# A constant row moved to PSUM in a gather-heavy graph layer

## The reference

```python
s_u = x @ W_u.T + b_u
s_v = x @ W_v.T
e = s_u[src] + s_v[dst]
e = jnp.where(e >= 0, e, 0.2 * e)
m = jax.ops.segment_max(e, dst, num_segments=n_nodes)
e_exp = jnp.exp(e - m[dst])
denom = jax.ops.segment_sum(e_exp, dst, num_segments=n_nodes)
probs = e_exp / denom[dst]
xh = x.reshape(n_nodes, head_dim, num_heads)
msg = xh[src] * probs[:, None, :]
out = jax.ops.segment_sum(msg, dst, num_segments=n_nodes)
```

## Time and profile before

| what | value |
|---|---|
| median of 3 runs | 4693.43 us (4681.35 to 4693.45) |
| profiled execution | 4686.26 us, its span 4684.5 us |
| POOL busy | 3468.7 us, 74% of the span |
| PE busy | 3095.6 us, 66% |
| DVE busy | 2213.4 us, 47% |
| mean granted TensorE clock | 0.814 of full |
| gathers of layer 1 (L1466) | 880, mean 1181 ns |

### The profile page before, as it was taken

How to read it: one execution, slowest core, us unless ns; L and a number is a source line. 1 busy time by engine, 2 the same in 40 slices (tenths; PEclk the granted TensorE clock), 3 DMA queues, 4 the chain that set the end, 5 groups by cost and what they waited for, 6 DMA issues and landing times. The chain is left out here.

```text
span 4684.5 us, 61408 instructions
## 1 busy us (share of the span) xinstructions
PE 3095.6 (66%) x13554; PEld 1900.7 (41%) x13555; DVE 2213.4 (47%) x5019; ACT 908.4 (19%) x2810; POOL 3468.7 (74%) x2948
## 2 busy tenths in 40 slices
PE   2548777877777777777777776884545555555541
PEld 1224444444444444444444443552333333443331
DVE  2553333333333333333333332995766667766665
ACT  0212222222222222222222222332000000000002
POOL 4237888888888888888888886775777777777764
PEclk9768888889888888888889897996777767667765
DMA  8667666667666667666667666565443434444431
GB/s 300 168 235 176 125 132 134 133 126 138 129 133 125 133 131 135 124 133 130 135 125 131 133 133 132 177 202 172 115 113 109 113 113 114 114 112 114 114 102 63
DMA packets 471759, 641.52 MB, mean 137 GB/s; under 512 B 173607, under 2 KB 365635, under 8 KB 467886
## 3 DMA queue, kind: packets, MB, share of 16 engines
q0 software_dynamic: 198144, 339.26, 38.1%
q1 hardware_dynamic: 245994, 254.83, 18.2%
q10 hardware_dynamic: 27588, 47.08, 3.1%
HBM read 448.23 MB, written 192.71 MB: 137 GB/s over the span
## 5 line engine op out<-in xcount | busy, mean ns | idle before, releaser
L935 POOL DMA_INDIRECT S<-l_msum,l_sink x784 | 1284.8, 1639 | 254.2 <-issue 213.0
L1466 POOL DMA_INDIRECT l_feats<-X_rows,l_gsrc x880 | 1039.2, 1181 | 326.9 <-issue 264.6
L918 POOL DMA_INDIRECT l_ga<-A_rows,l_gsrc x784 | 789.7, 1007 | 265.6 <-issue 160.0
L1008 PE MATMUL l_psU<-l_hid,l_same 128*128 128x257 f32 x1568 | 585.9, 459 | 535.6 <-ACT l_hid L1044 505.3
L981 PE MATMUL l_psC<-l_table,l_onehot 128*128 x4728 | 727.4, 295 | 0.0
L1532 PE MATMUL l_psU<-l_feats,l_same 128*128 128x264 f32 x1760 | 553.5, 478 | 169.5 <-DVE l_feats L1701 124.6
L1048 ACT COPY l_msum<-l_psU 128x257 f32<-128x257 f32 x784 | 292.6, 373 | 1889.9 <-POOLq L934 1313.6
L974 PE MATMUL l_psC<-W1cT,l_attrT 64*128 64x256 f32 x1576 | 623.4, 479 | 13.0 <-DMA l_table<-B_rows 13.0
L981 PEld LDWEIGHTS l_psC<-l_table,l_onehot 128*128 128x128 bf16 x4728 | 426.1, 104 | 367.9 <-issue 306.0
L1008 PEld LDWEIGHTS l_psU<-l_hid,l_same 128*128 128x128 f32 x1568 | 267.4, 214 | 666.2 <-ACT l_hid L1044 579.0
L1532 PEld LDWEIGHTS l_psU<-l_feats,l_same 128*128 128x128 f32 x1760 | 409.0, 240 | 306.9 <-issue 216.8
(11 more groups left out here) (346 smaller groups left out, 3390.7 us busy)
## 6 DMA issues: line engine op xcount, KB each, us to landing
l_srcb<-src_rows SPq DMA_DIRECT2D x99, 512.0 KB
l_locb<-lo_rows SPq DMA_DIRECT2D x55, 512.0 KB
S<-su_zeros ACTq DMA_DIRECT2D x24, 1156.5 KB
l_locb<-loc_rows SPq DMA_DIRECT2D x99, 256.0 KB
nd_sums<-S SPq DMA_DIRECT2D x196, 128.5 KB, 2.2
l_attr<-in_edge_attr SPq DMA_DIRECT2D x98, 256.0 KB
GH_rows<-l_hidden SPq DMA_DIRECT2D x49, 384.0 KB
nd_hidden<-GH_rows SPq DMA_DIRECT2D x49, 384.0 KB, 3.1
```

The source lines that it names most:

```text
L918: pool.indirect_dma_start(ga[:, s, :], None, D["A"], bass.IndirectOffsetOnAxis(ap=gsrc[h][:, j % HALF:j % HALF + 1], axis=0)).then_inc(gat ...
L935: pool.indirect_dma_start(D[f"S{j % NTAB}"], bass.IndirectOffsetOnAxis(ap=sink[j // HALF][:, j % HALF:j % HALF + 1], axis=0), msum[:, j % ...
L1008: nc.tensor.matmul(psU[j % 2][:, 0:UW], same[j // HALF][:, j % HALF, :], hid[:, j % RING, :], start=True, stop=True).then_inc(agg_done, 1)
L1466: pool.indirect_dma_start(feats[r][:, t, :], None, D["X1"], bass.IndirectOffsetOnAxis(ap=gsrc[r][:, t:t + 1], axis=0)).then_inc(gathered[r ...
```

## The change

The constant row is copied once, at the start of layer 1, from SBUF into the first 128 columns of a new PSUM bank `psW` (the eighth), and `find_edge` reads its first operand there. Its second operand, its output and its shape stay. The weight products (L1701) still read both operands from SBUF. Nothing else in the program is added, removed or put in another order; in the changed file the lines behind the new tile lie one to three further down.

```diff
--- before.py
+++ after.py
@@ -1388,6 +1388,7 @@
         psE = m.ps("psE", [P, 512])
         psM = m.ps("psM", [P, 512])
         psV = m.ps("psV", [P, 512])
+        psW = m.ps("psW", [P, 512])
         psU = [m.ps(f"psU{q}", [P, 512]) for q in range(4)]
         keys_in, tables_ready, table_split = m.sem("keys_in"), m.sem("tables_ready"), m.sem("table_split")
         loc_in = [m.sem(f"loc_in{r}") for r in range(SETS)]
@@ -1405,6 +1406,7 @@
         block = st.enter_context(nc.Block())
 
         ENDS, CARRY, SHRINK = P, P + 2 * GROUP, P
+        column = psW[:, 0:P]
 
         def groups(engine, body):
 
@@ -1578,7 +1580,7 @@
                 nc.vector.tensor_scalar(onehot[:, :, :], locb[r][:, :, :], K["winid"][:, 0:1], None, ALU.is_equal).then_inc(onehot_ready, 1)
 
             def find_edge(g):
-                nc.vector.tensor_tensor(same[:, :, :], K["column"][:, :].unsqueeze(1).to_broadcast([P, GROUP, P]),
+                nc.vector.tensor_tensor(same[:, :, :], column.unsqueeze(1).to_broadcast([P, GROUP, P]),
                                         K["loX"][:, bass.ds(g * GROUP, GROUP)].unsqueeze(2).to_broadcast([P, GROUP, P]),
                                         ALU.is_equal).then_inc(same_ready, 1)
 
@@ -1627,6 +1629,7 @@
             split_float(nc, first_steps, K["svf"][:, :, :], svrest[:, :, :],
                         [table[:, :, n * NH:(n + 1) * NH] for n in range(NSPLIT)])
             dve.sem_inc(table_split, 1)
+            nc.vector.tensor_copy(column, K["column"][:, :])
             nc.vector.memset(ones[:, :], 1.0)
             nc.vector.memset(forth[:, 0:1], LOW)
             nc.vector.memset(carry[:, 1, GROUP - 1:GROUP], LOW)
```

## The result

The changed kernel takes 4983.1 us (median of 4 runs, 4955.41 to 4992.98) against 4693.44 us (4 runs, 4681.35 to 4711.45): ratio 1.060, 95% interval 1.055 to 1.066. The forecast was 4668 us. It is slower by 6%, outside the range of 4640 to 4690 us, and on the side to which the prediction gave 0.07. One execution of the last experiment, h2, took 6009.6 us where the twelve others took 4686 to 4711; it is left out, and since it is the profiled one, h2 has no trace to read here.

What follows compares the result with a forecast made beforehand. In 28 groups the end of POOL's gathers narrowly set the pace, in 19 the DVE-PE-DVE chain. Copy 0, `find_edge` 0 and -18.8 us for the 28 groups took 4686.3 to 4667.5, so 4668 us; range 4640 to 4690.

Steps and rivals of the forecast that it cites:

- the side to which the prediction gave 0.07: Whole kernel: the chance given to a time slower by over 0.3%.
- The operation itself, the copy and the gathers: Layer 1: `find_edge` stays at 2.27 us, copy costs 0, gathers beside `find_edge` fall to 0.95 us.
- The counts of gathers in the prediction: Whole trace: 55 gathers begin beside L1581, 1.45 us longer on average; 111 beside L1611, none longer.
- The waits for gathers: DVE at `take_scores`: waits of 21.6, 1.1 and 9.9 us in the three stretches nearly vanish.
- The rise of POOL's spare time: POOL: one held gather a group goes, freeing 79.5 us; POOL waits more for PE instead.
- DVE and PE: what is late next is their own chain: Layer 1 loop: once gathers no longer bound it, this chain sets the period, 23.59 us; 18.8 us saved over 28 groups.
- by the middle stretch as it is: Loop's second stretch, hardly waiting for gathers: its 23.85 us bounds the new period from above, 11.5 us saved.
- late rises: PE's clock reaching 2.4 GHz at 12.5 us or later: the named reason if the period stays at 23.85 us or above.
- POOL's new rhythm hits DVE: Rival, chance 0.09: longer forms of L1672, L1686 and L1578 in all 55 groups add 28 us, giving 4696 us.
- without its two odd groups: Middle stretch: periods of 25.50 and 26.62 us, put down to single delays, left out to get 23.59 us.

Runs made afterwards that it cites:

- h2: Kernel before, with POOL waiting ahead of gather 10 of a group until the turn of `top` is complete: 4695.1 us, ratio 0.9997.
- e3: Changed kernel with the new bank and copy kept, but `find_edge` reading the column from SBUF again: 4698.1 us, ratio 1.0002.
- e1: Changed kernel, with POOL waiting ahead of the ninth of a group's 16 gathers until `find_edge` has ended: 4801.1 us, ratio 1.023.
- g1: Changed kernel, with POOL waiting ahead of gather 12 (t == 12) until the turn of `top` is complete: 4721.9 us, ratio 1.013.
- f5: Changed kernel with only 12 of the 16 gathers in every group after the second: 4695.2 us, ratio 1.0058.
- e2: Changed kernel with the second burst of eight score matmuls moved behind the turn of `top`: 4715.1 us, ratio 1.0055.
- f1: Changed kernel with the 16 score matmuls issued two at a time behind each pair of long sums, not in bursts: 4765.3 us, ratio 1.022.
- g3: Changed kernel with every gather reading 32 bytes instead of 1056 from each row: 4910.7 us, ratio 1.052.
- f6: Changed kernel with SP's load of 512 KB in each group cut to one row of 512 bytes: 4913.2 us, ratio 1.053.
- f3: Kernel before with every burst of eight score matmuls made twice over: 4684.6 us, ratio 1.0039.

## Why the prediction was wrong

*The operation itself, the copy and the gathers* were right: 2273 ns, nothing (e3: ratio 1.0002), and a gather that starts beside `find_edge` takes 0.95 us. The counts of gathers in the prediction are not exact: 52 and not 55 begin while L1581 runs, held by 1.53 us in the mean, which gives the same 79.5 us; and of the 65 that begin while L1611 runs one is longer, 1.96 us. *The waits for gathers* went as said. The rise of POOL's spare time was right in direction; it waits for PE.

*The step that failed* is "DVE and PE: what is late next is their own chain", and in it the bound from above, "by the middle stretch as it is". It took the chain of DVE and PE for a thing with a length of its own, which can only come nearer once POOL is out of the way. But the middle stretch had the held gather in it too, once in each group, and that hold was part of why its chain ran in 23.85 us. There was no row for the chain beside a train without that hold, so the bound had no ground on the slow side. What the runs showed in its place: without the hold PE's completions come late beside the train, DVE's wait for the turn went from 0.8 to 6.8 us a group, and the period from 24.1 to 30.3 us.

*The clock* is not the reason, though the prediction named late rises as the reason if the period stayed at 23.85 us or above. In the group of 4383.90 the granted clock does reach its upper level (2.4 GHz) only 19 to 20 us into it, but the turn is late ahead of that. DVE's waits ahead of the sums (L1613), where slower matmuls would show, are 252.3 us, and 260.1 before (L1611).

*The rivals* had the right subject once, "POOL's new rhythm hits DVE", and a reason close to what was found (L1581's end aligns POOL anew in each group). It priced only the longer forms of three short operations of DVE, 28 us. Those hardly moved: L1675, L1689 and L1580 together are busy for 79.3 us, and the same three lines of before (L1672, L1686 and L1578) for 78.3. The price was in the waits for PE, ten times as much.

*The rows that could have told it* were set aside as single delays: I took the middle stretch "without its two odd groups", and the stretches themselves leave out two longer ones, of 32.5 and 38.2 us. The longest starts at 4476.85. Its timeline:

```profile
4482.75 1.19 POOL L1466 DMA_INDIRECT l_feats<-X_rows,l_gsrc  x1 [0.30 <-issue]
...
4484.24 1.01 POOL L1466 DMA_INDIRECT l_feats<-X_rows,l_gsrc  x1 [0.30 <-issue]
4484.56 6.12 PE L1532 MATMUL l_psU<-l_feats,l_same 128*128 128x264 f32 x16 [3.18 <-issue]
...
4486.81 0.95 POOL L1466 DMA_INDIRECT l_feats<-X_rows,l_gsrc  x1 [0.30 <-issue]
4488.06 0.95 POOL L1466 DMA_INDIRECT l_feats<-X_rows,l_gsrc  x1 [0.30 <-issue]
4489.31 0.95 POOL L1466 DMA_INDIRECT l_feats<-X_rows,l_gsrc  x1 [0.30 <-issue]
4490.06 0.43 DVE L1611 TENSOR_TENSOR acc<-acc,l_psU 128x264 f32 x1 [2.90 <-PE l_psU L1532]
```

In the group of the earlier trace rows the first two weight products hold a gather for 1.69 us; here they meet only gathers of 1.19 and 1.01 us. A run of 0.95 us gathers follows, and DVE's sum waits 2.90 us, where 1.57 is usual. That looks like the regime of after in small, with the sums late in place of the turn; no run shows what makes one group odd and the next not.

*What is shown and what stays open.* Shown: the loss comes with the operand alone (e3); it lies in waits for PE's completions; it shrinks when POOL pauses (e1, g1), when the train is shorter (f5), or when no burst stands ahead of the turn (e2, f1); neither the gathers' data (g3) nor SP's load (f6) accounts for more than a sixth of it; a doubled burst is nearly harmless while the hold is there (f3). Open is by which path the gathers hold back what by the records PE has finished, whether by their issue or their packets, why the turn of e2 passes in the midst of a train, and how much of PE's work a train can take before it shows. SP's instructions, which are slow in the same stretches, were not taken away in any run. Not tried: pauses of fixed length.

## What to carry to other kernels

A stall that repeats in every period is part of the rhythm: before it is removed, look for what gets through during it, and price the loop without it on the slow side too. The odd periods of a trace are samples of another regime; read them before they are left out of a mean. With GpSimd issuing gathers back to back, it is worth trying to move bursts of short matmuls from ahead of a result that another engine waits for (e2 gave back nine tenths of a 6% loss by moving eight matmuls). And distrust a releaser that ended long before the wait did.

## What the runs showed of the hardware

- Beside a train of gathers (0.95 us each, one every 1.25 us), a transpose that ended was taken up by the waiting engine up to 8.9 us later (changed kernel; 11 us in e1), in 45 of the 51 late groups 1.2 to 3.0 us behind the end of the train's last gather. The semaphore of the burst of short matmuls ahead of it came 10.3 us behind the burst's end in the median (0.9 us in the kernel before).
- SyncE's own instructions are slower in such a train: the median of the register operation ahead of L1442 went from 41 to 700 ns (37 ns in e3, with the operand back in SBUF).
- One operand of a 128x2048 comparison moved from SBUF to PSUM left its duration at 2273 ns and freed the gathers beside it altogether (2.45 to 0.95 us).
- A gather of 32 bytes a row takes GpSimd 0.94 to 0.95 us beside no other hold (g3), as one of 1056 bytes does.
